# Mixture-of-experts stage of a macaron block: gate and up products turned, expert weights copied by ScalarE, token weights applied behind the down product

## The reference

```python
x = x + 0.5 * ffn(layernorm(x))     # layer 0: attention and experts
x = x + attn(layernorm(x))          # layer 1: attention alone
x = x + 0.5 * ffn(layernorm(x))     # layer 2: as layer 0
```

```python
weights = jnp.sum(jax.nn.one_hot(topi, E) * topv[..., None], axis=-2)   # 2 of 8 per token
gate = jnp.einsum('bsd,edm->bsem', h, w_gate)     # d = 128, m = 448
up   = jnp.einsum('bsd,edm->bsem', h, w_up)
act  = jax.nn.silu(gate) * up * weights[..., None]
moe  = jnp.einsum('bsem,emd->bsd', act, w_down)
```

## Time and profile before

| | |
|---|---|
| three runs, median | 1901.65 us |
| the profiled execution: its own time | 1902.52 us |
| its span, first to last instruction | 1900.9 us |
| busy in the span: PE, PEld, DVE, ACT, POOL | 88%, 38%, 73%, 56%, 23% |
| mean granted TensorE clock | 0.911 of 2.4 GHz |
| expert stage of layer 0 | about 556 to 698 us of the span |
| expert stage of layer 2 | about 1758 to 1901 us |
| lines 1133, 1151, 1142, 1118 in the chain that ended last | 3%, 2%, 1%, 0% |

### The profile page before, as it was taken

One profiled execution on the slowest core, in us unless ns is written; L12 is line 12 of the kernel. 1 busy time (PEld: TensorE's weight loads), 2 busy tenths in 40 slices (PEclk: granted clock), 3 DMA queues, 4 the chain that ended last, 5 costly groups with the idle time before them and its releaser, 6 DMA issues. The chain is left out here.

```text
span 1900.9 us, 30318 instructions
## 1 busy us (share of the span) xinstructions
PE 1678.3 (88%) x10566; PEld 720.8 (38%) x10566; DVE 1379.6 (73%) x2863; ACT 1073.4 (56%) x2301; POOL 444.9 (23%) x492
## 2 busy tenths in 40 slices
PE   4799999999749948899999999579999999993995
PEld 2333333333237723233333332233333333323674
DVE  8788899987153348888999983388899999826333
ACT  2355677677614413356777678234576777781442
POOL 6300201111016637000102020260011010200664
PEclk9788999999859967889999999678899999995898
DMA  4500203300011134200202000242002020001113
GB/s 130 118 21 3 51 3 99 71 2 2 8 33 41 43 103 139 52 1 2 52 2 52 3 2 2 60 139 52 2 12 42 2 52 2 2 2 30 38 43 88
DMA packets 63574, 75.83 MB, mean 40 GB/s; under 512 B 13655, under 2 KB 56220, under 8 KB 62104
## 3 DMA queue, kind: packets, MB, share of 16 engines
q1 hardware_dynamic: 54184, 62.13, 13.1%
q0 software_dynamic: 4992, 9.40, 2.0%
q10 hardware_dynamic: 4224, 2.10, 0.4%
HBM read 53.05 MB, written 21.46 MB: 39 GB/s over the span
## 5 line engine op out<-in xcount | busy, mean ns | idle before, releaser
L753 ACT ACTIVATE probs<-ps 128x512 f32<-128x512 f32 (+3 forms) x1920 | 879.1, 542 | 473.0 <-PE ps L861 471.6
L604 DVE TENSOR_REDUCE mpart<-ps 128x1 f32<-128x512 f32 (+3 forms) x1680 | 1015.1, 666 | 117.3 <-PE ps L815 65.5
L815 PE MATMUL ps<-ka,qa 96*128 96x512 bf16 (+3 forms) x1920 | 669.9, 371 | 36.4 <-DMA ka<-ksplit 23.6
L861 PE MATMUL ps<-qa,ka 96*128 96x512 bf16 (+3 forms) x1920 | 616.1, 357 | 3.1 <-DMA qa<-guard 2.5
L874 PE MATMUL ps<-probs,vv 128*9 128x512 f32 (+3 forms) x3840 | 441.8, 532 | 8.8 <-ACT probs L753 8.1
L702 POOL TENSOR_SCALAR_AFFINE_SELECT probs<-probs 128x512 f32<-128x512 f32 x192 | 121.8, 634 | 1180.0 <-ACT probs L753 1180.0
L815 PEld LDWEIGHTS ps<-ka,qa 96*128 96x128 bf16 x1920 | 191.9, 100 | 480.7 <-DVE mpart L604 338.6
L861 PEld LDWEIGHTS ps<-qa,ka 96*128 96x128 bf16 x1920 | 183.6, 100 | 189.0 <-ACT probs L753 69.2
L818 PE MATMUL ps<-mask_rows,identb 128*128 128x128 bf16 x768 | 161.4, 235 | 0.0
L1212 DVE SCALAR_TENSOR_TENSOR probs<-probs,slot_w,ps 128x448 f32<-128x448 f32 x78 | 53.1, 680 | 117.2 <-PE ps L1133 113.7
L874 PEld LDWEIGHTS ps<-probs,vv 128*9 128x9 f32 x3840 | 57.7, 88 | 157.8 <-ACT probs L753 116.4
(11 more groups left out here) (170 smaller groups left out, 1092.8 us busy)
## 6 DMA issues: line engine op xcount, KB each, us to landing
qa<-qsplit SPq DMA_DIRECT2D x27, 384.0 KB
ka<-ksplit SPq DMA_DIRECT2D x27, 384.0 KB
probs<-rope SPq DMA_DIRECT2D x12, 512.0 KB, 6.7
qa<-qsplit SPq DMA_DIRECT2D x36, 96.0 KB
ka<-ksplit SPq DMA_DIRECT2D x36, 96.0 KB
qsplit<-arena SPq DMA_DIRECT2D x6, 384.0 KB, 3.2
ksplit<-arena SPq DMA_DIRECT2D x6, 384.0 KB, 2.8
tokens<-arena SPq DMA_DIRECT2D x2, 1024.0 KB, 7.4
```

The lines of the kernel that those rows point to most:

```text
L604: dve.tensor_reduce(mpart[:, j % MD, h0:h0 + some, qt, kc], ps[:, bank, 0:some * w].rearrange("p (h w) -> p h w", h=some), axis=AX.X, op=A ...
L753: act.activation(probs[:, s % 2, h, 0:n], ps[:, u % SB, 0:n], ACT.Exp, scale=SCALE).then_inc(probs_ready, 1)
L815: ins = pe.matmul(dst, qa[0:KROWS, b, h0 + k, tile * 128:(tile + 1) * 128], ka[0:KROWS, b, h0 + k, kc * CH:kc * CH + n], start=True, stop= ...
L861: pe.matmul(dst, ka[0:KROWS, b, h, kt * 128:(kt + 1) * 128], qa[0:KROWS, b, h, c * CH + q0:(c + 1) * CH], start=True, stop=True).then_inc( ...
```

## The change

Gate and up are computed the other way round: 112 columns of the expert's weights are the stationary operand, the turned tile (128 tokens) is the moving one. The results have the inner channels on partitions, as the down product wants them, and the four transposes (line 1142) and the copy of their result (line 1179) are gone. The stationary operand lies in a fixed buffer: ScalarE reads the expert's number, copies gate and up weights of the slot's expert (128x896, now side by side in one tensor `wgu`) to one of two fixed buffers (`wcur`), and TensorE waits for `expert_copied`. The token's weight now varies along the columns of the activations, so it is applied to the output of the down product, where tokens are on partitions again. The pipeline is one stage shorter: pass `i` has gate and up of `i` and the down product of `i-1`, which now has two PSUM banks.

```diff
@@ buffers
-    wgs = sb("wgs", [128, E, M])
-    wus = sb("wus", [128, E, M])
+    wgu = sb("wgu", [128, E, 2 * M])
-    sgb = [pflat[:, i * CH:i * CH + M] for i in (0, 1)]
-    acb = [pflat[:, i * CH:i * CH + M] for i in (2, 3)]
-    atb = [pflat[0:MR, i * CH:(i + 1) * CH].rearrange("p (c t) -> p c t", c=MC) for i in (4, 5)]
+    sgb = [pflat[0:MR, i * CH:(i + 1) * CH] for i in (0, 1)]
+    atb = [pflat[0:MR, i * CH:(i + 1) * CH] for i in (2, 3)]
+    wcur = pflat[:, 4 * CH:4 * CH + 4 * M].rearrange("p (b m) -> p b m", b=2)
@@ TensorE
                     turn(0)
-                    for i in range(NSLOT + 2):
-                        if i + 1 < NSLOT:
+                    for i in range(NSLOT + 1):
+                        if 1 <= i and i + 1 < NSLOT:
                             turn(i + 1)
                         if i < NSLOT:
+                            pe.wait_ge(expert_copied, i + 1)
                             pe.wait_ge(tile_copied, i + 1)
                             if i >= 2:
                                 pe.wait_ge(act_ready, i - 1)
-                            for k, w in ((0, wgs), (1, wus)):
-                                pe.matmul(ps[:, 2 * (i % 2) + k, 0:M], xt[:, i % 2, :],
-                                          w[:, bass.ds(expert, 1), :].rearrange("p o m -> p (o m)"),
-                                          start=True, stop=True).then_inc(gate_up_ready, 1)
-                        if 1 <= i <= NSLOT:
+                            for b in (0, 1):
+                                for k in range(MC):
+                                    ins = pe.matmul(ps[0:MR, 2 * (i % 2) + b, k * 128:(k + 1) * 128],
+                                                    wcur[:, i % 2, b * M + k * MR:b * M + (k + 1) * MR],
+                                                    xt[:, i % 2, :], start=True, stop=True)
+                                ins.then_inc(gate_up_ready, 1)
+                        if i == 0:
+                            turn(1)
+                        if i >= 1:
                             u = i - 1
                             pe.wait_ge(act_ready, u + 1)
                             if u >= 2:
-                                pe.wait_ge(act_copied, u - 1)
+                                pe.wait_ge(out_copied, u - 1)
                             for k in range(MC):
-                                ins = pe.transpose(ps[0:MR, 4 + u % 2, k * 128:(k + 1) * 128],
-                                                   acb[u % 2][:, k * MR:(k + 1) * MR], identf[:, :])
...
-                                ins = pe.matmul(ps[:, 6, 0:D], atb[u % 2][:, k, :],
+                                ins = pe.matmul(ps[:, 4 + u % 2, 0:D], atb[u % 2][:, k * 128:(k + 1) * 128],
@@ ScalarE
+                    def copy_expert(u):
+                        expert = act.value_load(eti[0:1, u:u + 1], min_val=0, max_val=E - 1)
+                        if u >= 2:
+                            act.wait_ge(gate_up_ready, 2 * (u - 1))
+                        act.activation(wcur[:, u % 2, :], wgu[:, bass.ds(expert, 1), :].rearrange("p o m -> p (o m)"),
+                                       ACT.Copy).then_inc(expert_copied, 1)
+
+                    act.wait_ge(weights_loaded, 64)
+                    copy_expert(0)
                     copy_turned(0)
-                    for i in range(NSLOT + 1):
+                    for i in range(NSLOT):
                         if i + 1 < NSLOT:
                             copy_turned(i + 1)
-                            act.activation(sgb[i % 2], ps[:, 2 * (i % 2), 0:M], ACT.Silu).then_inc(silu_ready, 1)
-                            act.wait_ge(act_turned, u + 1)
...
-                            act.activation(atb[u % 2], ps[0:MR, 4 + u % 2, :].rearrange("p (c t) -> p c t", c=MC),
-                                           ACT.Copy).then_inc(act_copied, 1)
+                            copy_expert(i + 1)
+                        act.activation(sgb[i % 2], ps[0:MR, 2 * (i % 2), :], ACT.Silu).then_inc(silu_ready, 1)
@@ VectorE
+                        if u:
+                            dve.wait_ge(weight_found, u)
...
-                            dve.scalar_tensor_tensor(acb[i % 2], sgb[i % 2], slot_w[:, i % XR:i % XR + 1],
-                                                     ps[:, 2 * (i % 2) + 1, 0:M], ALU.mult, ALU.mult).then_inc(act_ready, 1)
+                            dve.tensor_tensor(atb[i % 2], sgb[i % 2], ps[0:MR, 2 * (i % 2) + 1, :],
+                                              ALU.mult).then_inc(act_ready, 1)
                             if i + 1 < NSLOT:
                                 weight(i + 1)
-                        if i >= 2:
-                            u = i - 2
+                        if i >= 1:
+                            u = i - 1
+                            dve.wait_ge(weight_found, u + 1)
                             dve.wait_ge(down_ready, u + 1)
-                            dve.tensor_copy(obuf[:, u % OR, :], ps[:, 6, 0:D]).then_inc(out_copied, 1)
+                            dve.tensor_scalar(obuf[:, u % OR, :], ps[:, 4 + u % 2, 0:D], slot_w[:, u % XR:u % XR + 1], None,
+                                              ALU.mult).then_inc(out_copied, 1)
```

More of the change, by code:

```diff
@@ L333, in macaron_kernel @@
     tile_copied = sem("tile_copied")
+    expert_copied = sem("expert_copied")
     gate_up_ready = sem("gate_up_ready")
@@ L502, in _ @@
                         load_first(c - 1)
-                bulk = [(rts[:, :], router), (wgs[:, :, :], w_gate.rearrange("e d m -> d e m")),
-                        (wus[:, :, :], w_up.rearrange("e d m -> d e m")),
+                bulk = [(rts[:, :], router), (wgu[:, :, 0:M], w_gate.rearrange("e d m -> d e m")),
+                        (wgu[:, :, M:2 * M], w_up.rearrange("e d m -> d e m")),
                         (wds[0:MR, :, :, :], w_down.rearrange("e (c p) d -> p e c d", p=MR))]
@@ L1122, in _ @@
                     experts = []
-                    for i in range(NSLOT + 2):
-                        if i + 1 < NSLOT:
+                    for i in range(NSLOT + 1):
+                        if 1 <= i and i + 1 < NSLOT:
                             turn(i + 1)
                         if i < NSLOT:
-                            expert = pe.value_load(eti[0:1, i:i + 1], min_val=0, max_val=E - 1)
-                            experts.append(expert)
+                            experts.append(pe.value_load(eti[0:1, i:i + 1], min_val=0, max_val=E - 1))
+                            pe.wait_ge(expert_copied, i + 1)
                             pe.wait_ge(tile_copied, i + 1)
@@ L1139, in _ @@
                             if u >= 2:
-                                pe.wait_ge(act_copied, u - 1)
+                                pe.wait_ge(out_copied, u - 1)
                             for k in range(MC):
-                                ins = pe.transpose(ps[0:MR, 4 + u % 2, k * 128:(k + 1) * 128],
-                                                   acb[u % 2][:, k * MR:(k + 1) * MR], identf[:, :])
-                            ins.then_inc(act_turned, 1)
-                        if i >= 2:
-                            u = i - 2
-                            pe.wait_ge(act_copied, u + 1)
-                            if u:
-                                pe.wait_ge(out_copied, u)
-                            for k in range(MC):
-                                ins = pe.matmul(ps[:, 6, 0:D], atb[u % 2][:, k, :],
+                                ins = pe.matmul(ps[:, 4 + u % 2, 0:D], atb[u % 2][:, k * 128:(k + 1) * 128],
                                                 wds[0:MR, bass.ds(experts[u], 1), k, :].rearrange("p o d -> p (o d)"),
@@ L1164, in _ @@
                 with act.If(layer != 1):
+                    def copy_expert(u):
[6 more added lines that the diff above has]
+                    copy_expert(0)
                     copy_turned(0)
[L1166 removed]
+                    for i in range(NSLOT):
                         if i + 1 < NSLOT:
                             copy_turned(i + 1)
[L1169 to L1180 removed]
+                            copy_expert(i + 1)
+                        act.wait_ge(gate_up_ready, 2 * i + 1)
+                        if i >= 2:
+                            act.wait_ge(act_ready, i - 1)
+                        act.activation(sgb[i % 2], ps[0:MR, 2 * (i % 2), :], ACT.Silu).then_inc(silu_ready, 1)
                     for k in range(OR):
```

15 lines of the change are left out of this document (1 added, 14 removed).

## The result

| | kernel before | changed kernel |
|---|---|---|
| median, us | 1901.08 (1900.13 to 1904.47, 4 runs) | 1886.99 (1885.49 to 1888.54, 4 runs) |
| ratio to before, 95% interval | | 0.9922 [0.9906, 0.9938] |
| profiled execution, span | 1902.52, 1900.9 | 1885.49, 1883.9 |
| TensorE busy | 1678.3 | 1660.7 |

What follows compares the result with a forecast made beforehand. TensorE's stream was taken to bound the expert stages. Per stage 6.1 (period) - 3.0 (filling) + 2.3 (draining) = 5.4 us, twice 10.9, taking the profiled 1902.52 to 1891.6 and the median to 1890.8 us; range 1884 to 1899.

Steps and rivals of the forecast that it cites:

- period: TensorE's time per steady slot of an expert stage: 2.95 to 2.78 us, gaining 6.1 us per stage over 36 periods.
- filling: Start of each expert stage until slot 2: a loss of 3.0 us per stage, between 1.5 and 3.9.
- draining: End of each expert stage, slot 38 to the last output: 6.78 to 4.45 us, a gain of 2.3.
- 16 x 0.111: New gate and up on TensorE: 16 passes at the down product's 0.111 us, 1.78 us per slot.
- Open loads: Rival: weight loads of the 16 passes not hidden, 0.107 us more each, 111 us in all, 2013 us; chance 0.02.
- 571.4 in place of 570.7: Start of slot 2 in the filling: 570.7, or 572.3 if the clock stays low through slot 1; 571.4 taken.
- The hop from the weight copy to TensorE: Delay from ScalarE's weight copy to TensorE's gate and up: between 0.04 and 0.78 us, taken as 0.25.
- The pause of 2 us: In the filling, TensorE idles some 2 us before slot 1, waiting for turn 1, tile copy, read and weight copy.
- the lower bound: Smallest gain in the drain: 1.95 us per stage in place of 2.3, if the last scatter queues.
- ScalarE's loop, the main rival: Tile copy, read and weight copy in series set the period and the kernel is slower, 1910.3 us at 3.05; chance 0.10.
- GpSimd: Rival: scatter and gather, 2.92 us a slot if the 0.63 before each scatter is needed, set the period; 1901; chance 0.03.
- A late clock: Rival: after the filling's pause two more slots per stage run at half clock, costing 11 us, 1901.7; chance 0.06.

Runs made afterwards that it cites:

- e9: e8's kernel with the down product's last chunk contracted over 128 rows in place of 64, the added weight rows zeroed; 1873.1 us, ratio 0.9847 to the kernel before.
- e8: e7's kernel with gate and up in seven products of 128 stationary columns in place of eight of 112; 1894.9 us, ratio 0.9964 to the kernel before.
- e7: Changed kernel with tile 1 turned between gate and up of slot 0 and slot 1's weights copied right behind slot 0's; 1881.91 us, ratio 0.9894.
- e10: Changed kernel with ScalarE copying each slot's expert weights twice, e3's kernel on a third chip; 1894.06 us, ratio 0.9967 to the kernel before.
- e11: Kernel before with only the token's weight moved from the multiply to the down product's output; 1902.01 us, ratio 0.9995 to the kernel before.
- e6: Kernel before, unaltered, run again on a second chip; 1901.76 us in a single run.
- e1: Same kernel as e7 (changed kernel, pipeline filled in another order) on the first, disturbed chip; 1919.55 us, ratio 0.9994 to the kernel before.
- e3: Changed kernel with ScalarE copying each slot's expert weights twice, on the first, disturbed chip; 1939.32 us, ratio 1.0109 to the kernel before.
- e5: Changed kernel, unaltered, run again on a second chip; 1887.72 us, ratio 0.9924 to the kernel before.
- e4: Changed kernel with each gate and up product issued as two of 64 moving columns, 32 passes in place of 16; 2022.27 us, ratio 1.0536.

## Why the prediction was right, and where its sizes were off

Right in direction and mechanism, and 3.8 us too high in the number (1890.8 forecast, 1886.99 measured). All three terms erred to the same side, by little each. Term by term, per stage:

| term | predicted | measured |
|---|---|---|
| period | 2.95 to 2.78, 6.1 us | 2.944 to 2.750, 7.0 us |
| filling | 3.0 lost | 1.8 to 1.9 lost |
| draining | 2.3 gained | 2.35 gained |
| sum, two stages | 10.9 | 7.0 - 1.85 + 2.35 = 7.5, twice 15.0 (the stages: 14.9; medians: 14.1) |

**Period.** The step "16 x 0.111" took the down product's 128 stationary columns. The new passes have 112, as the transposes had, and cost 0.1094, close to the transposes' 0.110, which stands in the forecast as a bound from below. The down product, unchanged, stays at 0.89/8 = 0.111, and e9's gate and up, with 128 stationary columns and nothing else changed in them, cost 1.56/14 = 0.111 too: a pass does depend a little on the stationary columns. That is worth 16 x 0.0016 = 0.026 us a slot, 0.9 us per stage.

**Open loads.** Ruled out: PEld is busy in every microsecond of the steady stretch and PE waits for none. The Trainium skill ("TensorE: Matmul & The Clock Gate", Part 3, "The mechanism") would have a load overlap matmuls in flight only between different row groups. The rows disagree: sixteen loads of 128 rows behind one another are hidden, and so are the down product's of 112 rows between them. What stood open, 0.34 us a slot, was a product of 64 rows among products of 128 (e8 against e9).

**Filling.** This term was mis-sized, by 1.15 us a stage. The largest part is the clock: the forecast went 0.7 us above its own sum (571.4 in place of 570.7) for a clock that stays low into slot 1; it rose in slot 0. Two smaller parts stand in the timeline above. The weight copy was put 1.0 us behind the start of the tile's copy, for the read of the expert's number; since the read runs beside that copy, it starts 0.64 us behind it (561.83 to 562.47). The hop from the weight copy to TensorE was put at 0.25, but from 562.47 + 0.95 = 563.42 to 563.48 it is 0.06. The path was not quite right either: slot 2 was forecast to wait for its weight copy, but that ended at 566.33, and what held TensorE was the wait for VectorE before the first down product. The pause of 2 us itself is as forecast, and e7 shows that it, and not the copy, was the price: with turn 1 back in its place both are to be had, and the filling is 1.0 us shorter than before the change.

**Draining.** 4.43 for 4.45. The last scatter queues at 0.30 behind the one before, as the lower bound had it.

**ScalarE's loop, the main rival.** Not near: the copy took 0.95 (0.94 forecast), but the read leaves 0.37 open and not 1.0, so 0.8 us are to spare where I gave 0.1 to 0.4. e10 loads ScalarE by another 0.85 us, and the period moves by only 0.05. **GpSimd**: the 0.63 was indeed the wait for VectorE; its floor, 2.60 (e9), lies under 2.75. **VectorE**: worth nothing, by e11. **A late clock**: in the changed kernel the contrary came, a clock up in slot 0. The forecast's argument against this rival, that the stream is dense again from slot 1 on, holds for e10 too, where the clock fell, so it isn't what kept it up here: that was luck in part. A low clock in slot 1 cost 0.5 us a stage there, where the rival had priced two whole slots, 5.6 us.

## What to carry to other kernels

Price a product by its passes and take the pass from the row with the same shape: the wrong number of columns was 0.9 us a stage here. When one engine's stream bounds a loop and the others have room, moving a re-layout (here four transposes) into a copy on an idle engine was free in the steady state, and its whole price was in the filling, where nothing hides it: look there for a better order (5.8 us here) before judging the edit. When a product is cut into fewer, wider chunks, look at the rows of the last one: seven chunks with one of 64 rows were 13 us slower than eight, and with that one padded to 128 rows about 9 us faster.

## What the runs showed of the hardware that was not expected

**The clock rose at different times for different work on TensorE.** From the first gate and up of a stage to the full clock it took 5.4 to 5.8 us in all six expert stages of the old orientation (the kernel before, e6, e11), 3.15 to 3.4 in all eighteen of the new one (the changed kernel, e1 to e3, e5 and e7 to e10), and 16.8 and 40.9 in the two stages of e4. Stretches of the kernel before, columns as in the earlier trace rows:

```profile
561.90:564.90 3.00, 2.93 (x4) 1.41 (x5) 0.00 (x0) 1.70 (x2) 2.09 (x3) 0.50 0.20 44
564.90:567.90 3.00, 3.00 (x7) 1.41 (x6) 0.76 (x3) 0.82 (x2) 0.73 (x1) 0.59 0.18 44
```

And of e4:

```profile
1830.00:1850.00 20.00, 20.00 (x106) 20.00 (x106) 2.23 (x8) 4.75 (x8) 5.92 (x6) 0.50 0.08 18
1853.00:1856.00 3.00, 3.00 (x30) 3.00 (x30) 0.00 (x0) 1.55 (x2) 1.98 (x2) 0.93 0.06 22
```

In the changed kernel the clock was up 3.15 us after the first gate and up; in e4 TensorE worked through the whole of the 20 us shown at 0.50. What makes the difference is open. It isn't the chip: e1 to e3 ran on e4's.

**The clock can fall again in the filling.** In e3 and e10, where TensorE idled 1.78 us before slot 1, it fell back to 0.50 within that slot, in all four stages; in the changed kernel and e5, with 0.93 us in the same place, in none.

**A product of 64 rows among products of 128 costs.** It makes itself and the turn behind it 0.34 us longer in sum (e8), though fewer rows are worked on. It isn't every change of row count: in the changed kernel the down product has 112 rows between products of 128, and it stays at 0.89 and the turn behind it at 0.11.

**One chip was slower than the others with every kernel**, the kernel before among them (1919.48 against 1901 to 1903), and in three of the four traces from it ScalarE and VectorE started late, ScalarE's tile copy by 0.6 to 2.5 us in 18 to 34 of 78 slots. The excess lies in the expert stages alone: e1's took 137.7 and 136.4 us where e7, the same kernel, took 116.2 and 116.1, which is 41.9 of the 44.2 us by which the two spans differ. No trace of the kernel before was taken there, so whether it was delayed in the same way isn't known, nor is the cause. It hid the whole improvement of about 1% that the same kernel shows elsewhere (e1 against e7), so no ratio from that chip enters the reasons above; of e4 only the steady slot does.

Not tried: a stationary operand picked by a register straight from the weights, which would take the copy away altogether.
